# One TensorE-bound attention and feed-forward layer: the preparation and the first iteration in another order

## The reference

```python
z = layernorm(x)                                   # per token, over 256 features
q, k, v = cproj(Wq), cproj(Wk), cproj(Wv)          # complex: 16 heads x 64, real and imaginary part
phase = complex(cos(ang), sin(ang))                # ang = t * omega, per head and channel
qr, kr = q * phase, k * phase                      # rotation
s = einsum('bihd,bjhd->bhij', qr, conj(kr)).real
qn, kn = squared norms of q and k
mu = sigmoid(mu_raw) + EPS
E = exp(clip(-mu * |i - j|, -30, 0))               # depends on head and distance alone
V = sigma_sq / (2 mu) * (1 - E*E) + eta_sq + gamma_sq      # softplus of raw constants
maha = max(qn + E*E * kn - 2 E * s, 0) / V
logits = coef * log1p(maha / nu) - 0.5 * DH * log(V)
A = softmax(where(causal, logits, -inf))
y = (A @ v, real and imaginary part) @ Wo
x = x + layernorm(y)
x = x + layernorm(silu(x' @ wg) * (x' @ wu) @ wd)  # x' = layernorm(x), integer weights / 127
```

## Time and profile before

| | |
|---|---|
| median of 3 runs | 1927.41 us (1927.08 to 1930.81) |
| the profiled execution, its own time | 1924.56 us |
| its span | 1922.6 us |
| TensorE matmul busy | 1796.9 us (93%) |
| VectorE busy | 1613.3 us (84%) |
| ScalarE busy | 1574.2 us (82%) |
| GpSimd busy | 1456.1 us (76%) |
| DMA, mean over the span | 61 GB/s |

### The profile page before, as it was taken

The page is one execution under the profiler, slowest core; times in us unless marked ns, Lnnn a source line. Parts: engine busy times, 40 slices in busy tenths (PEclk is TensorE's granted clock), DMA queues, the critical chain, the costliest instruction groups (busy, mean ns, idle before and its releaser), DMA issues.

```text
span 1922.6 us, 40883 instructions
## 1 busy us (share of the span) xinstructions
PE 1796.9 (93%) x10660; PEld 1476.0 (77%) x10660; DVE 1613.3 (84%) x3845; ACT 1574.2 (82%) x3217; POOL 1456.1 (76%) x1289
## 2 busy tenths in 40 slices
PE   2669999999999999999999999999999999998997
PEld 1447878888788877887888787878888788876876
DVE  6769888888888887888888888888888888896884
ACT  3478988888888887888888888898888888886654
POOL 3457788888888887888888887888888888772663
PEclk7779999999999999999999999999999999999998
DMA  7121211121113110131123110311131100110111
GB/s 216 61 88 75 76 44 45 51 92 51 45 45 110 61 45 33 69 93 45 45 78 93 45 45 25 109 61 45 45 109 44 45 34 34 44 45 23 44 45 44
DMA packets 61038, 117.70 MB, mean 61 GB/s; under 512 B 13440, under 2 KB 42880, under 8 KB 52656
## 3 DMA queue, kind: packets, MB, share of 16 engines
q1 hardware_dynamic: 60080, 115.51, 17.9%
q10 hardware_dynamic: 768, 0.00, 0.0%
HBM read 99.64 MB, written 21.36 MB: 63 GB/s over the span
## 4 chain that ended last, share of the span: by engine, by line
PE 61%; DVE 10%; POOL 6%; issue 5%; ACT 2%; DVEq 0%; POOLq 0%; ACTq 0%
PE pa L761 13%; PE ps L801 11%; PE py L825 11%; PE po L836 9%; PE pp L791 7%; PE pp L813 5%; POOL qk L592 4%; PE pa L772 3%; PE pa L780 2%; DVE lg L1518 2%; DVE stats L1556 1%; DVE lg L1526 1%; DVE ps L1507 1%; DVE acc L1578 1%; POOL ek L602 1%
## 5 line engine op out<-in xcount | busy, mean ns | idle before, releaser
L592 POOL TENSOR_TENSOR qk<-rm 64x512 f32<-64x512 f32 x512 | 694.6, 1357 | 121.6 <-PE ps L801 43.9
L602 POOL TENSOR_TENSOR ek<-tabs,kn 128x512 f32<-128x512 f32 (+3 forms) x512 | 461.2, 908 | 162.5 <-DVE lg L1518 112.5
L761 PE MATMUL pa<-xt,wt 128*128 128x512 f32 x1488 | 423.7, 421 | 30.5 <-DVE rm L1493 19.3
L1526 DVE CUSTOM_DVE_ANT_0 lg<-lg,tabs,ncog 128x512 f32<-128x512 f32 (+3 forms) x512 | 442.8, 883 | 0.0
L1493 DVE TENSOR_TENSOR rm<-pa,tabs 128x512 f32<-128x512 f32 x512 | 332.4, 677 | 68.8 <-POOL qk L592 64.6
L801 PE MATMUL ps<-qk 128*128 128x512 f32 (+3 forms) x1024 | 375.8, 451 | 14.1 <-DVE lg L1518 12.4
L1518 DVE CUSTOM_DVE_ANT_0 lg<-ps,ek,qb 128x512 f32<-128x512 f32 (+3 forms) x512 | 279.1, 545 | 126.8 <-POOL ek L602 81.4
L825 PE MATMUL py<-pt,vt 128*128 128x128 f32 x2560 | 347.8, 275 | 0.1
L825 PEld LDWEIGHTS py<-pt,vt 128*128 128x128 f32 x2560 | 330.8, 191 | 16.2 <-issue 0.3
L761 PEld LDWEIGHTS pa<-xt,wt 128*128 128x128 f32 x1488 | 275.4, 192 | 84.2 <-issue 27.9
L1132 ACT ACTIVATE lg<-lg,qb 128x512 f32<-128x512 f32 (+3 forms) x512 | 278.3, 558 | 25.9 <-DVE lg L1518 22.7
(11 more groups left out here) (181 smaller groups left out, 2190.9 us busy)
## 6 DMA issues: line engine op xcount, KB each, us to landing
xt<-xs_d SPq DMA_DIRECT2D x56, 1024.0 KB, 4.8
tabs<-vec_d SPq DMA_DIRECT2D x8, 1536.0 KB, 8.8
xs_d<-xt SPq DMA_DIRECT2D x6, 1024.0 KB, 3.9
wt<-wraw_d SPq DMA_DIRECT2D x7, 768.0 KB, 5.6
acc<-in_L_attn_x SPq DMA_DIRECT2D x8, 512.0 KB, 7.6
tabs<-in_L_attn_x SPq DMA_DIRECT2D x8, 512.0 KB, 4.7
out<-tabs SPq DMA_DIRECT2D x8, 512.0 KB, 3.1
tabs<-rope_d SPq DMA_DIRECT2D x56, 64.0 KB, 4.2
```

Of the source, the lines that this page charges most:

```text
L592: pool.tensor_tensor(qk[part * DH:(part + 1) * DH, z * HH + hh, :], rm[row, 2 * part, :], rm[row, 2 * part + 1, :], ALU.add if part else A ...
L602: pool.tensor_tensor(ek[:, n % 2, 0:w], tab(par, hh, E2_T, w), kn[:, hh, 0:w], ALU.mult).then_inc(ek_pool, 1)
L761: last = mm(pa[r][:, :], wproj(par, z, kt, a, r * P, (r + 1) * P), xbuf[x][:, kt, b, :], start=(n == 0), stop=(n == 3 * KT - 1))
L1526: dve.tensor_tensor_reduce(lg[:, hh, at(n)], lg[:, hh, at(n)], tab(par, hh, T3_T, w), ncog[:, par, 0, hh:hh + 1], 3e38, ALU.add, ALU.min, ...
```

## The change

Nothing is computed differently; instructions move on all engines but GpSimd, and one buffer (`ang3`) is new.

- Loads: the six loads of raw constants go from SP's queue to ScalarE's, ahead of the small omega loads; the four large omega loads go behind the first two activations. The load of `nco` stands ahead of the load of the decay tables.
- ScalarE: `group_trig` and the first two squares stand ahead of the two table logarithms. All of `rope_trig` moves to iteration 0, behind the exponentials up to head 1, tile 0. `ffn_keep(4)` to `(8)` move into iteration 0.
- VectorE: the first rotation stands among the table steps, ahead of the wait for `nco`, which moves behind the second rotation. `x_normal(1)` moves among the table steps, `x_stats(1)` behind the tables. Angle 1 leaves the preparation; `x_stats(3)` and angles 1 to 3 stand further back in iteration 0.
- TensorE: FFN turns 4 to 8 move into iteration 0, and the wait ahead of the third score goes.
- SP: `rope_store(0)` goes to the other three.

```diff
@@ buffers of the angles and their sines @@
+        ang3 = sb("ang3", [P, N])
-        ang = [pt[:, 0, :], yt[:, 1, :], pt[:, 0, :], spare[:, 2 * N:3 * N], yt[:, 1, :]]
-        prs = flat(pr[:, :, :])
-        rope_cs = [prs[:, 0:N], tabs[1][:, 0, :], tabs[1][:, 3, :], tabs[1][:, 6, :]]
...
+        ang = [pt[:, 0, :], yt[:, 1, :], spare[:, 2 * N:3 * N], ang3[:, :], yt[:, 1, :]]
+        rope_cs = [tabs[1][:, 0, :], tabs[1][:, 3, :], tabs[1][:, 6, :], tabs[1][:, 0, :]]
...
@@ sync @@
             x_load(1)
-            for k in range(5):
-                sp.dma_start(hp[:, k:k + 1], raw_d[k].rearrange("(h a) -> h a", a=1)).then_inc(p_load, 16)
-            sp.dma_start(hp[:, 5:6], tau_d.rearrange("(h a) -> h a", a=1)).then_inc(p_load, 16)
             stage_weights()
...
             sp.wait_ge(vec_out, 64)
+            sp.dma_start(nco[:, :, :], bass.AP(tensor=nco_d.tensor, offset=0, ap=[[0, P], [3, H], [1, 3]])).then_inc(nco_in, 16)
             load_decay(0, 0)
-            sp.dma_start(nco[:, :, :], bass.AP(tensor=nco_d.tensor, offset=0, ap=[[0, P], [3, H], [1, 3]])).then_inc(nco_in, 16)
             load_output_weights(0)
             x_store(0)
             x_store(1)
-            rope_store(0)
...
                 if t == 0:
-                    for k in range(1, ROPES):
+                    for k in range(ROPES):
                         rope_store(k)
@@ tensor, iteration @@
                     project(cn, it.behind, 1 - it.slot, it.xn, half, it.own, 0, 0)
+                if it.own == 1:
+                    ffn_turn(4)
+                    ffn_turn(5)
...
                     project(cn, it.behind, 1 - it.slot, it.xn, half, it.own, 0, 1)
+                if it.own == 1:
+                    for n in range(6, 9):
+                        ffn_turn(n)
@@ tensor, preparation @@
-            for n in range(6):
+            for n in range(4):
                 ffn_turn(n)
             norms_k(c0)
             scores(c0, 0, 0)
             norm_q(c0)
             scores(c0, 0, 1)
-            for n in range(6, 9):
-                ffn_turn(n)
             pe.wait_ge(w_lo, 3 * KT)
-            pe.wait_ge(ffn_ev, 9)
             scores(c0, 0, 2)
@@ scalar, preparation @@
+            for k in range(5):
+                act.dma_start(hp[:, k:k + 1], raw_d[k].rearrange("(h a) -> h a", a=1)).then_inc(p_load, 16)
+            act.dma_start(hp[:, 5:6], tau_d.rearrange("(h a) -> h a", a=1)).then_inc(p_load, 16)
...
-            for k in range(ROPES):
-                act.dma_start(om[:, k:k + 1], omega_d[4 * k:4 * k + 4, :].rearrange("a (d e) -> (a d) e", e=1)).then_inc(om_in, 16)
             act.wait_ge(p_load, 16 * 6)
             a_step(act.activation(hp[:, 6:11], hp[:, 0:5], ACT.Abs))
             a_step(act.activation(hp[:, 11:16], hp[:, 6:11], ACT.Exp, scale=-1.0))
+            for k in range(ROPES):
+                act.dma_start(om[:, k:k + 1], omega_d[4 * k:4 * k + 4, :].rearrange("a (d e) -> (a d) e", e=1)).then_inc(om_in, 16)
...
             x_high(0, 1)
-            act.wait_ge(p_dve, V_LN)
-            a_step(act.activation(v_lnv, v_v, ACT.Ln))
-            a_step(act.activation(v_t3, v_vn, ACT.Ln))
+            head_logs()
             group_trig()
...
             square(c0, 0, 0)
             square(c0, 0, 1)
+            act.wait_ge(p_dve, V_LN)
+            a_step(act.activation(v_lnv, v_v, ACT.Ln))
+            a_step(act.activation(v_t3, v_vn, ACT.Ln))
             ffn_cast_of(0)
             ffn_cast_of(1)
             square(c0, 1, 0)
             square(c0, 1, 1)
             x_high(1, 0)
             x_high(1, 1)
+            ffn_cast_of(2)
             ffn_keep(0)
             ffn_keep(1)
             ffn_keep(2)
-            ffn_cast_of(2)
             ffn_keep(3)
-            ffn_keep(4)
-            ffn_keep(5)
-            rope_trig(0)
             act.wait_ge(ncog_dve, 1)
             keep_norm_k(c0, 0, 0)
@@ scalar, iteration @@
...
-                if it.own == 1:
-                    rope_trig(1)
-                    rope_trig(2)
-                    rope_trig(3)
-                    act.wait_ge(rope_out[0], 48)
...
                 exp(c, 1, 0)
                 keep_values(c, it.slot, 1)
+                if it.own == 1:
+                    for k in range(ROPES):
+                        rope_trig(k)
+                    act.wait_ge(rope_act, 4 * ROPES + 3)
                 log(c, 1, 3, it.slot)
@@ vector, preparation @@
...
             step(tt(col(22), col(21), col(TAU), ALU.mult))
+            first_rotation()
             step(ts(v_v, v_v, col(C1), col(C2), ALU.mult, ALU.add))
...
@@ vector, iteration @@
                 logits(c, 0, 3, it.par)
-                if it.own == 1:
-                    x_stats(3)
-                    rope_angle(2)
-                    rope_angle(3)
...
                     rotate(cn, it.behind, 1, IC)
+                if it.own == 1:
+                    x_stats(3)
+                    rope_angle(1)
+                    rope_angle(2)
+                    rope_angle(3)
```

More of the change, by code:

```diff
@@ L1219, in body @@
                 log(c, 0, 3, it.slot)
+                if it.own == 1:
+                    ffn_keep(6)
+                    ffn_keep(7)
+                    ffn_keep(8)
                 if old:
@@ L1297, in _ @@
             log(c0, 0, 1, 0)
-            for n in range(6, 9):
-                ffn_keep(n)
             run_iterations(act, body)
@@ L1393, in rope_angle @@
                 z = ang[k]
-                if k in (1, 2):
-                    dve.wait_ge(rope_act, 4 * k - 1)
-                if k == 3:
+                if k == 1:
+                    dve.wait_ge(rope_act, 3)
+                if k == 2:
                     dve.wait_ge(ffn_tr, 9)
@@ L1408, in x_low, with rotate, first_rotation @@
                    ALU.subtract).then_inc(x_lo, 1)
+            c0 = counts(dve, 0, (8, 4, 2, 1))
+            def rotate(c, par, z, m):
+                r = m in (IS, IC)
+                dve.wait_ge(sq_act, c[4] + 2 * z + r + 1)
+                for h in range(HH):
+                    dve.wait_ge(rot_pool[h], c[4] + (1 + (m in (RS, IC)) if z else 0))
+                tt(rm[:, m, :], pa[r][:, :], ropet(par, m in (IS, RS)), ALU.mult).then_inc(mul_dve, 1)
+            def first_rotation():
+                dve.wait_ge(rope_act, 3)
+                rotate(c0, 0, 0, RC)
+                rotate(c0, 0, 0, IS)
+                rotate(c0, 0, 0, RS)
+                rotate(c0, 0, 0, IC)
             def x_move(a):
@@ L1456, in _ @@
             x_low(0, 1)
-            x_stats(1)
+            dve.wait_ge(p_act, 3)
+            step(ts(col(39), col(35), 2.0, None, ALU.mult))
+            step(rec(col(39), col(39)))
+            step(tt(v_e2, v_e, v_e, ALU.mult))
+            step(ts(v_e, v_e, -2.0, None, ALU.mult))
+            step(ts(v_v, v_e2, -1.0, 1.0, ALU.mult, ALU.add))
             step(ts(col(21, 5), col(0, 5), 0.0, None, ALU.max))
@@ L1481, in _ @@
             step(ts(col(RB), col(25), -BIG, None, ALU.mult))
+            x_normal(1)
             dve.wait_ge(p_act, 6)
@@ L1485, in _ @@
             assert done[0] == V_TABLES, done
-            def rotate(c, par, z, m):
-                r = m in (IS, IC)
-                dve.wait_ge(sq_act, c[4] + 2 * z + r + 1)
-                for h in range(HH):
-                    dve.wait_ge(rot_pool[h], c[4] + (1 + (m in (RS, IC)) if z else 0))
-                tt(rm[:, m, :], pa[r][:, :], ropet(par, m in (IS, RS)), ALU.mult).then_inc(mul_dve, 1)
             def bounds(c, par, slot):
@@ L1712, in start @@
                 settle(v)
-            dve.wait_ge(nco_in, 16)
-            dve.wait_ge(consts, 9)
-            start(0, 0)
-            c0 = counts(dve, 0, PERS)
-            rotate(c0, 0, 0, RC)
-            rotate(c0, 0, 0, IS)
-            rotate(c0, 0, 0, RS)
-            rotate(c0, 0, 0, IC)
-            x_normal(1)
+            x_stats(1)
             x_low(1, 0)
             x_low(1, 1)
-            x_move(1)
             rotate(c0, 0, 1, RC)
@@ L1729, in _ @@
             rotate(c0, 0, 1, IC)
+            dve.wait_ge(nco_in, 16)
+            start(0, 0)
+            x_move(1)
             rope_angle(0)
             x_stats(2)
-            rope_angle(1)
             dve.wait_ge(grp[0], 16 * TABLE_LOADS)
```

20 lines of the change are left out of this document (9 added, 11 removed).

## The result

The changed kernel took 1910.45 us (median of 4 runs, 1905.7 to 1911.88) beside 1928.66 for the kernel before (4 runs on the same chip, 1927.08 to 1930.81): a ratio of 0.9901, 95% interval [0.9880, 0.9921], so 15 to 23 us less. Forecast were 22.1 less, and 1905.3. The profiled execution took 1910.13 with a span of 1908.3.

What follows compares the result with a forecast made beforehand. TensorE was taken to bound the kernel from 135 us, so only an earlier end of iteration 0 counts. The chain through the front and iteration 0 gained 22.1 us: 1927.41 - 22.1 = 1905.3, range 1899 to 1915.

Steps and rivals of the forecast that it cites:

- Up to the first projection: nothing: Start of the kernel: the twelve projection matmuls end at 25.3 us as before, with an omega delay of 0.
- omega lands late: Rival: the moved omega loads delay everything by up to 5.6 us, giving 1910.9; chance 0.08.
- The first rotation and the tables: VectorE's front: first rotation ends at 27.8, 17 us earlier; table steps end at 33.2, two us later.
- GpSimd is late next: GpSimd's queue ahead of the second rotation: power ends 38.4, rotation sums 45.2 against 49.4, a gain of 4.2 us.
- The first decay: VectorE's first decay multiply in the preparation comes at 55.2 us, against 67.66 before.
- The third decay: VectorE's wait of 5.78 us behind a score matmul goes; the decay comes at 58.1, 18.2 us earlier.
- The turns in iteration 0: Five FFN turns and five ScalarE copies added there cost 3.0 us, between bounds of 0 and 5.5.
- Block and sines: Late iteration 0: `x_stats(3)` 4.6 us and three angles at 2.95 each end at 95.6; ScalarE's logarithm at 99.3.
- Angles and powers collide: Rival in iteration 0's block: each angle takes 4.9 us beside GpSimd, 5.8 less gain, 1911.1; chance 0.14.
- The marker follows the same chain: VectorE's decay at 125.47, first narrow one of iteration 1, follows the chain that brings the logarithm 22.1 us earlier.
- the slower rival: TensorE's clock stays at its lower level past iteration 0: +10 us, 1937; chance 0.02.
- After that: nothing: Past iteration 0 both programs have the same queues, so nothing further is gained or lost.

Runs made afterwards that it cites:

- experiment 1: The changed kernel run and profiled once more, nothing altered: 1911.12 us, ratio 0.9910 to the kernel before.
- experiment 3: The changed kernel with the four large omega loads issued again ahead of ScalarE's first activations: 1908.81 us, ratio 0.9899.
- Experiment 4: The changed kernel with GpSimd's `x_rstd(1)` moved behind its first four rotation sums: 1906.23 us, ratio 0.9891.
- experiment 2: The kernel before run and profiled a second time, nothing changed: 1929.15 us, ratio 0.9998.
- sines back (6): The changed kernel with angles, sines and `x_stats(3)` back in their old places: 1921.62 us, ratio 0.9963.
- front alone (7): The changed kernel with FFN turns, angles and sines back in their old places; loads, constants and front order stay new: 1925.93 us, ratio 0.9984.
- omega and power (8): The changed kernel with omega loads ahead of the activations and `x_rstd(1)` behind GpSimd's first four rotation sums: 1903.64 us, ratio 0.9871.
- all three (10): The changed kernel with omega loads ahead, `x_rstd(1)` behind the first sums and angle 0 in iteration 0's block: 1903.38 us, ratio 0.9869.
- experiment 5: The changed kernel with all nine FFN turns and the wait for their copies back in the preparation: 1914.03 us, ratio 0.9926.
- experiment 9: The changed kernel with angle 0 moved from the preparation into the block of angles in iteration 0: 1909.37 us, ratio 0.9890.

## Why the prediction was right, and where its steps were off

The sign, the mechanism and the main term held. The point forecast is 5 us below the median measured, inside the range of 1899 to 1915. The gain of 22.1 lies within the interval of the first measurement (15 to 23 us) but outside that of experiment 1 (14 to 20 us), so it was somewhat too large. That it came this near is luck in part: the logarithm at which the sum ended came 3.3 us later than forecast, what is left of errors of +5.2 and -2.5 and of smaller ones, and the marker then gained 2.0 more than the logarithm for a reason that the forecast did not have.

*Up to the first projection: nothing.* This step failed, and by a sign that the forecast had named, a wait for omega at 14. The last omega load was issued at 10.1 (forecast 9.5) and took 6.2 to land, not the 4.4 of the earlier trace rows; VectorE stood for 2.49. It is the rival "omega lands late", at less than half its upper bound; by experiment 3 it costs 1.5 us at the end. The 4.4 had been read from loads of which the last was issued at 4.5; why the one of 10.1 took 6.2 no run here settles. The 2.6 us by which the two activations put off the issue (7.5 in experiment 3) are about the wait. The Trainium skill (DMA: Bandwidth & Descriptors, Issuing engines are not separate DMA queues) says that another issuing engine saves only the time of issuing. The trace agrees for the six constants, which took 4.7 us to land (median) from ScalarE's queue and 4.2 from SP's. Omega never changed its queue, only its place in it, so that rule does not explain its delay, although the prediction drew on it there.

*The first rotation and the tables.* Forecast ends 27.8 and 33.2; measured 30.5 and 35.8. Of these 2.6 to 2.7 us omega makes 1.9: in experiment 3, with omega on time, the two ends are 28.6 and 33.8. The other 0.7 is the first projection, reckoned to end at 25.3 as before: its twelve matmuls took 5.42 us, not 4.83, and in experiment 3 5.46. `x_normal(1)` cost 1.38 (33.28), as priced. The table load took 9.9 us and not 7.9, so the tables landed at 48.9 where 44 was forecast; here nothing waited for them.

*GpSimd is late next.* Right, and the most useful step: the power, the sums and the second rotation were forecast at 38.4, 45.2 and 46.5 and ended at 41.1, 47.7 and 49.1, again 2.5 to 2.7 late throughout. The first rotation ended 14.5 us earlier than before (30.5 against 45.0), the sums of GpSimd only 1.7 (47.7 against 49.4). Experiment 4 shows that the queue's order held the sums up by 12.5 us, but also that this order hid only 3.8 us at the marker: behind it stand the slower table steps and `nco`.

*The first decay: 60.19, not 55.2.* 2.6 come with the rotation. The others are two terms beside GpSimd: angle 0 took 6.4 (50.30 to 56.69), where the forecast had 4.9 from the old place, and `x_move`, which the sum had left out, took 1.1 (49.19 to 50.30). The old 4.9 was no price of an angle beside GpSimd but that of one with part of its passes beside it.

*The third decay.* The 5.78 went entirely (0.25 left). Right.

*The turns in iteration 0, 3.0 between bounds of 0 and 5.5.* Mis-sized: 0.4. TensorE and ScalarE had room there. From the third decay to the end of `logits` took 14.7 (to 78.1), 0.5 more than before, not 17.2; this gave back half of what omega, angle 0 and `x_move` had cost. Errors of +5.2 and -2.5 so met in a total that looks better than its terms.

*Block and sines.* The stretch in front took 7.4 (forecast 6.8), the block 13.3 (13.45), and the logarithm stood 3.8 behind the block's end (forecast 3.7). The block hides two errors that met: `x_stats(3)` took 3.5 and not 4.6, and angle 1 took 3.9 and not 2.95.

*Angles and powers collide.* It did not happen: the statistics (2.70) and the first passes of angle 1 (0.43, 0.75) ran at their old durations beside the two powers (3.49 us on GpSimd from 87.44), where the prediction's use of the rule had let the powers block VectorE for 3.2 us. What cost 0.9 us was a product of GpSimd (`ek<-tabs,kn`, from 90.89): one pass of angle 1 took 1.37 beside it.

*The marker follows the same chain.* It does not. It gained 20.8, the logarithm 18.8. The marker waits for TensorE (1.02 in front of it), and TensorE's second scores of iteration 1 came 21.0 us earlier. Before:

```profile
120.55 1.63 PE L801 MATMUL ps<-qk 128*128 128x384 f32 x2
```

In the changed kernel this row stands at 99.51. In the old program TensorE came to it in one run from 114.09, behind the exponentials, with 6.5 us of turns, norms and first scores at half the clock (0.50 from 114 to 120). In the changed kernel that work is done by 90.3, beside VectorE's block, and the second scores follow the block's end by 0.7. From the second scores to the marker it took 4.9 us before and 5.15 after, so this stretch gained nothing. The clock is alike in both: before it was at half up to 123 and back by 124, in the changed kernel it is back by 103, so 1.5 to 2.5 us ahead of the marker each time. The window before:

```profile
120.00:123.00 3.00, 3.00 (x10) 2.23 (x10) 1.77 (x5) 2.85 (x5) 1.19 (x3) 0.50 0.00 0
```

After:

```profile
99.00:103.00 4.00, 3.49 (x9) 2.51 (x10) 3.72 (x11) 3.94 (x7) 2.73 (x3) 0.52 0.89 333
103.00:107.00 4.00, 4.00 (x27) 3.47 (x26) 2.28 (x9) 3.83 (x9) 2.05 (x3) 1.00 0.75 218
```

So the slower rival, a clock that stays low past iteration 0, did not come: the granted clock is 1.00 from 103 on.

*After that: nothing.* Right between the two profiles that compare like with like (experiment 2), but not shown for the medians. Single executions of one kernel differ by much: the 21 runs of before beside experiment 2 went from 1922.78 (mean clock 0.980) to 1933.51 (0.974). Yet in every comparison the median gained less than the marker (us; markers against the 125.47 of the first profile, medians against those of the kernel before in the same comparison):

| version | marker earlier by | median less by |
|---|---|---|
| the change | 20.8 | 18.2 |
| the change again (1) | 20.6 | 15.9 |
| omega ahead (3) | 22.3 | 18.2 |
| power behind (4) | 24.6 | 20.8 |
| turns back (5) | 15.9 | 14.2 |
| sines back (6) | 8.0 | 5.4 |
| front alone (7) | 4.0 | 2.3 |
| omega and power (8) | 27.3 | 24.6 |
| angle 0 in the block (9) | 23.0 | 19.4 |
| all three (10) | 26.5 | 25.4 |

So by the medians 1 to 5 us are given back on the way. A likely place is the hole of experiment 2: in the profiles the clock fell behind it in one of the two of before, but in nine of the ten of the changed versions. The nine runs of the changed kernel also lie in two groups, two at 1905.4 and 1905.7 and seven from 1910.1 to 1911.9, about as far apart as the two places cost. That the changed order makes the clock fall more often is not shown, since the other executions have no trace, but it is not excluded either; it is the rest of Theory B.

## What to carry to other kernels

When a wait is removed, follow the released work to the next engine's queue before counting it: here the first rotation ended 14.5 us earlier, and all of the front was worth 4. GpSimd had a late instruction ahead of the sums; moving that one behind them gave 3.8 us more, and then the next waits took over. Work that only later parts need (angles, sines, weight transposes) belongs behind the first work that fills the bound engine; that was 17 of the 21 us. And price the parts of such a change by an early marker in the trace that repeats to a few tenths, not by the spans of two profiles, which can differ by 6 us with nothing changed. What reaches the end only the medians say, and here it was 1 to 5 us less.

## What the runs showed of the hardware

- **Which VectorE passes suffer beside GpSimd's sums.** `x_stats` (one input in SBUF) took 2.70 beside them and without them. The rotation, with one input in PSUM, took 2.63 and 2.47 for four. Passes with two SBUF inputs went from 0.75 to 1.63, and single-input `tensor_scalar` passes of 128x512 from 0.43 to 1.37 or 1.10. An instruction of 0.15 took 0.94. The extra 0.7 to 1.0 us is about the same for a pass of 0.43, 0.75 and 0.15, so it goes by what GpSimd has in work, not by the size of the waiting pass. The Trainium skill (SBUF — State Buffer, Who interferes with whom) draws this line: one SBUF input outside the two-port modes does not contend, two inputs or a two-port mode do. All these rows agree.
- **Not all GpSimd work blocks.** Beside its two powers on 128x8 (3.49 us in all) a pass of angle 1 with two SBUF inputs kept its 0.75, and a `tensor_scalar` its 0.43. Taken by the letter the rule above would have had them wait; the measurement decides.
- **A standing hole can end either way.** The same program at the same place, 1159 us, kept its clock once and fell to half of it once, with holes of 3.31 and 3.55 us. Together with the end of attention this made 5.8 us between two profiles of one program. The length of the hole does not decide it alone: behind 3.19 us (experiment 5) and 3.23 us (experiment 1) the clock fell, behind 3.57 us (experiment 9) it did not. What does stays open.
